# Attention transposed by VectorE in 32x32 blocks with an exchange through DRAM, in a two-layer graph network on one core

## The reference

```python
u = jnp.einsum('bid,bjd->bij', h, h) / temper
a = jax.nn.softmax(u, axis=-1)
delta = a * adjacency_matrix
attn = delta / (jnp.sum(delta, axis=-1, keepdims=True) + 1e-10)
hl = h @ wl.T + b_l
hs = h @ ws.T + b_s
hr = h @ wr.T + b_r
diag_a = jnp.diagonal(attn, axis1=1, axis2=2)
ctx = einsum('bij,bjd->bid', attn * upper, hl) + diag_a[..., None] * hs + einsum('bij,bjd->bid', attn * lower, hr)
o = (ctx - mean) / jnp.sqrt(var + LN_EPS) * g + beta
return relu(o)
```

## Time and profile before

| | |
|---|---|
| median of 3 runs | 1699.22 us (1698.93 to 1699.52) |
| the profiled execution | 1699.16 us, its span 1697.4 us |
| busy share PE, DVE, POOL, ACT | 98%, 84%, 67%, 52% |
| instructions | 34570 |
| TensorE's granted clock, mean | 0.994 of full speed |
| DMA | 97.63 MB in 93905 packets |

### The profile page before, as it was taken

The page is one execution under the profiler, slowest core; times in us unless marked ns, Lnnn a source line. Parts: engine busy times, 40 slices in busy tenths (PEclk is TensorE's granted clock), DMA queues, the critical chain, the costliest instruction groups (busy, mean ns, idle before and its releaser), DMA issues.

```text
span 1697.4 us, 34570 instructions
## 1 busy us (share of the span) xinstructions
PE 1670.7 (98%) x10112; PEld 1652.4 (97%) x10112; DVE 1429.1 (84%) x4496; ACT 882.3 (52%) x2182; POOL 1131.2 (67%) x1798
## 2 busy tenths in 40 slices
PE   7999999999999999999999999999999999999996
PEld 7999999999999999999999999999999999999995
DVE  6888888888888888888888888888888888888887
ACT  4555545554555555455545554555555455545553
POOL 2666676666666666766666666667676666666663
PEclk9999999999999999999999999999999999999998
DMA  4112111111111121111111111111121111111111
GB/s 166 49 52 62 51 57 53 59 53 55 59 54 57 51 61 51 57 52 61 51 57 58 55 57 51 59 54 57 51 62 51 57 57 56 56 52 57 56 46 39
DMA packets 93905, 97.63 MB, mean 58 GB/s; under 512 B 10688, under 2 KB 92864, under 8 KB 93888
## 3 DMA queue, kind: packets, MB, share of 16 engines
q1 hardware_dynamic: 93888, 97.43, 18.5%
HBM read 72.22 MB, written 25.17 MB: 57 GB/s over the span
## 4 chain that ended last, share of the span: by engine, by line
PE 97%; DVE 1%; ACT 0%; issue 0%; DMA 0%; POOL 0%; SPq 0%; DVEq 0%; POOLq 0%; ACTq 0%
PE p_proj L305 71%; PE p_gather L363 16%; PE p_score L299 5%; PE p_gather L385 2%; PE p_attnT L344 2%; PE p_score L337 1%; DMA w_raw<-WT 0%; DVE p_gather L437 0%; DVE proj L462 0%; DVE w L496 0%; DVE stats L406 0%; DVE y L443 0%; ACT w L607 0%; ACT proj_split L587 0%; POOL rstd L671 0%
## 5 line engine op out<-in xcount | busy, mean ns | idle before, releaser
L305 PE MATMUL p_proj<-w,hT_layer 128*128 128x384 f32 x6912 | 1406.6, 344 | 0.2 <-DVE w L496 0.2
L305 PEld LDWEIGHTS p_proj<-w,hT_layer 128*128 128x128 f32 x6912 | 1153.7, 189 | 9.5 <-DVE w L496 0.7
L667 POOL TENSOR_TENSOR attnT_split<-attnT,attnT_split 128x256 fp32r<-128x256 f32 x256 | 189.4, 740 | 449.2 <-DVE rows L481 442.4
L215 POOL TENSOR_TENSOR proj_split<-proj,proj_split 128x768 fp32r<-128x768 f32 x252 | 465.2, 1846 | 5.3 <-issue 5.3
L591 ACT ACTIVATE normed<-gathered,nbias,rstd 128x384 f32<-128x384 f32 x128 | 90.7, 709 | 443.7 <-POOL nbias L675 443.7
L363 PE MATMUL p_gather<-proj_split,attnT_split 128*128 128x384 f32 x1536 | 310.9, 337 | 7.8 <-DVE y L443 4.3
L363 PEld LDWEIGHTS p_gather<-proj_split,attnT_split 128*128 128x128 f32 x1536 | 271.9, 189 | 8.4 <-issue 6.1
L462 DVE TENSOR_TENSOR proj<-p_proj,bias_all 128x768 f32<-128x768 f32 x256 | 243.6, 951 | 6.0 <-PE p_proj L305 5.9
L671 POOL TENSOR_TENSOR rstd<-veps,neg_half 128x1 f32<-128x1 f32 x384 | 210.6, 548 | 49.9 <-DVE neg_mean L420 27.9
L582 ACT ACTIVATE attnT_split<-attnT 128x256 fp32r<-128x256 f32 x256 | 105.0, 410 | 243.5 <-DVE attnT L488 243.5
L299 PE MATMUL p_score<-hT_layer 128*128 128x256 f32 x768 | 215.6, 283 | 5.0 <-POOL hT_layer L707 5.0
(11 more groups left out here) (48 smaller groups left out, 1679.3 us busy)
## 6 DMA issues: line engine op xcount, KB each, us to landing
xt_raw<-xT SPq DMA_DIRECT2D x128, 192.0 KB, 2.4
xn<-x SPq DMA_DIRECT2D x128, 192.0 KB, 2.4
out<-o SPq DMA_DIRECT2D x128, 192.0 KB, 1.9
adj_layer<-adj SPq DMA_DIRECT2D x256, 64.0 KB, 1.9
w_raw<-WT SPq DMA_DIRECT2D x6, 576.0 KB, 7.4
bias_all<-bias SPq DMA_DIRECT2D x2, 576.0 KB, 9.0
gain<-gain_row SPq DMA_DIRECT2D x1, 192.0 KB, 9.6
shift<-shift_row SPq DMA_DIRECT2D x1, 192.0 KB, 9.9
```

The source lines that it names most:

```text
L215: op.tensor_tensor(proj_split[k][:, LO], proj[k][:, UP:LOW + 1, :], proj_split[k][:, HI].bitcast(F32), ALU.subtract).then_inc(s_proj_lo[k], 1)
L305: return nc.tensor.matmul(p_proj[:, which, 0:D], hT[k][:, slot, st, c, :], w[:, k, which, mv, c, :], start=(n == 0), stop=(n == 8))
L667: nc.gpsimd.tensor_tensor(AT_split[k][:, LO], AT[k][:], AT_split[k][:, HI].bitcast(F32), ALU.subtract).then_inc(s_side_lo[k], 1)
```

## The change

The attention is no longer transposed by TensorE, except for the very last graph's layer 2 (`direct`). `mask` is followed on VectorE by `nc.vector.transpose`, which transposes each 32x32 block within `A` in place of the whole, into `A_blocks`; the diagonal is taken from `A` right there. SP stores `A_blocks` to a DRAM scratch and loads it back in four DMAs, one for each group of 32 partitions, with the blocks exchanged, into `AT_whole`. The cut into sides moves from VectorE to GpSimd. Layer 1's normalised rows are still transposed by TensorE, into a bank `p_rows` of their own. Around this, the order of the work changes on every engine: VectorE's output rows go from the end of an iteration (graph i - 3) to just behind layer 1's normalisation (graph i - 4), layer 2's sides and the score matmuls move, and GpSimd's order is new.

The core of the diff:

```diff
+        def direct(i, b):
+            return isinstance(i, int) and b == G - 1
...
+            def store_attn(k, b, slot):
+                done(sp, s_attn_blocks[k], b)
+                sp.dma_start(attn_mem[k][slot], A_blocks[k][:]).then_inc(s_attn_out[k][slot], 16)
+
+            def load_attn(k, b, slot):
+                moved_and_done(sp, s_attn_out[k], b, slot, s_side[k])
+                blocks = attn_mem[k][slot].rearrange("(r a) (s b) -> s a r b", a=B, b=B)
+                for s in range(4):
+                    sp.dma_start(AT_whole[k][s * B:(s + 1) * B, :].rearrange("a (r b) -> a r b", b=B),
+                                 blocks[s]).then_inc(s_attn_in[k][slot], 16)
...
             def iteration(i, p):
                 q = 1 - p
+                if live(i, i):
+                    load_attn(0, i, p)
...
+                if live(i, i - 2) and not direct(i, i - 2):
+                    store_attn(1, i - 2, p)
...
+                if live(i, i - 2) and not direct(i, i - 2):
+                    load_attn(1, i - 2, p)
...
+                if live(i, i + 1):
+                    store_attn(0, i + 1, q)
...
-                    done(pe, s_attn[k], b)
-                    nc.tensor.transpose(p_attnT, A[k][:], ident[:]).then_inc(s_attnT[k], 1)
+                    if k == 1 and direct(i, b):
+                        done(pe, s_attn[k], b)
+                        nc.tensor.transpose(p_attnT, A[k][:], ident[:]).then_inc(s_attnT, 1)
...
-                project_and_score(i, 0, i, p, 1, i - 2, p, i - 3)
+                project_and_score(i, 0, i, p, 1, i - 2, p, i - 3, 4, 16)
...
-                project_and_score(i, 1, i - 2, p, 0, i + 1, q, i)
+                project_and_score(i, 1, i - 2, p, 0, i + 1, q, i, 0, 8)
...
+                done(dve, s_attn[k], b)
+                if not apart:
+                    nc.vector.transpose(A_blocks[k][:], A[k][:]).then_inc(s_attn_blocks[k], 1)
+                nc.vector.tensor_tensor_reduce(diag_scratch[k][:], A[k][:], ident_p[k], 1.0, 0.0, ALU.mult,
+                                               ALU.add, col(rows[k], slot, DIAG)).then_inc(s_diag[k], 1)
...
                 if live(i, i - 1):
                     normalise_layer1(i, q)
+                if live(i, i - 4):
+                    output_rows(i, p)
...
-                if live(i, i - 3):
-                    output_rows(i, q)
...
+            def cut_sides(k, b, slot):
+                gathered_in(pool, s_attn_in[k], b, slot)
+                nc.gpsimd.tensor_tensor(AT[k][:], AT_whole[k][:].unsqueeze(1).broadcast_to([P, 2, N]), sides[:],
+                                        ALU.mult).then_inc(s_side[k], 1)
...
+                if live(i, i - 1):
+                    deviation_layer1(i - 1)
                 if live(i, i - 3) and not by_vector(i, 1, i - 3):
                     low_projections(nc.gpsimd, pool, 1, i - 3)
-                if live(i, i - 4):
-                    deviation_output(i - 4)
-                if live(i, i - 1):
-                    deviation_layer1(i - 1)
+                if live(i, i):
+                    cut_sides(0, i, p)
                 if live(i, i + 1):
                     low_input(i + 1, q)
                 if live(i, i - 2):
                     done(pool, s_attn[1], i - 2)
                 if live(i, i):
                     low_sides(0, i)
+                if live(i, i - 4):
+                    deviation_output(i - 4)
```

More of the change, by code:

```diff
@@ L326, in project_and_score @@
                         last = project_step(k, slot, UP + n // 9, n % 9)
-                    if score and n % 2 == 0 and n // 2 < C:
-                        step = score_step(other, slot_other, n // 2)
-                        if n // 2 == C - 1:
+                    if score and n == first:
+                        done(pe, s_lo[other], b_other)
+                        done(pe, s_diag[other], b_other - 1)
+                    if score and n >= first and (n - first) % 2 == 0 and (n - first) // 2 < C:
+                        step = score_step(other, slot_other, (n - first) // 2)
+                        if (n - first) // 2 == C - 1:
                             step.then_inc(s_parts[other], 1)
@@ L333, in project_and_score @@
                         gather(k, b_gather)
-                    if score and n == 14:
+                    if score and n == last_part:
                         done(pe, s_cross[other], b_other)
@@ L501, in _ @@
             nc.vector.tensor_copy(ident_r[:], ident[:]).then_inc(s_ident_r, 1)
+            for k in range(2):
+                nc.vector.tensor_copy(ident_p[k], ident[:]).then_inc(s_ident_p, 1)
+            dve.wait_ge(s_ident_p, 2)
             dve.wait_ge(s_w[0][UP], 16)
@@ L592, in normalise, with relu_rows @@
                                      scale=rstd[:, which:which + 1]).then_inc(s_rows, 1)
+            def relu_rows(i, b, slot):
+                if isinstance(i, int) and i == 1:
+                    act.wait_ge(s_const, 64)
+                done(act, s_normedT, b)
+                for c in range(C):
+                    last = nc.scalar.activation(relu_T[:, c, :], relu_T[:, c, :], ACT.Relu,
+                                                bias=shift1[:, c:c + 1], scale=gain1[:, c:c + 1])
+                last.then_inc(s_relu, 1)
+                done(act, s_relu, b)
+                done(act, s_self[1], b - 2)
+                nc.scalar.activation(hT[1][:, slot, HI], relu_T, ACT.Copy).then_inc(s_hi[1], 1)
             def finish(i, p):
@@ L619, in iteration @@
                     high_input(i + 1, q)
-                if live(i, i - 2):
+                if live(i, i - 3) and not direct(i, i - 3):
+                    high_sides(1, i - 3)
+                if live(i, i - 2) and not last_graph(i):
                     cross_scores(1, i - 2)
@@ L624, in iteration @@
                     normalise(0, gathered[:], normed[:], s_normed)
-                if live(i, i):
-                    high_sides(0, i)
+                if live(i, i - 2) and last_graph(i):
+                    cross_scores(1, i - 2)
                 if live(i, i - 2):
@@ L635, in iteration @@
                 if live(i, i - 1):
-                    if isinstance(i, int) and i == 1:
-                        act.wait_ge(s_const, 64)
-                    done(act, s_normedT, i - 1)
-                    for c in range(C):
-                        last = nc.scalar.activation(relu_T[:, c, :], relu_T[:, c, :], ACT.Relu,
-                                                    bias=shift1[:, c:c + 1], scale=gain1[:, c:c + 1])
-                    last.then_inc(s_relu, 1)
-                    done(act, s_relu, i - 1)
-                    done(act, s_self[1], i - 3)
-                    nc.scalar.activation(hT[1][:, q, HI], relu_T, ACT.Copy).then_inc(s_hi[1], 1)
-                if live(i, i - 2):
-                    high_sides(1, i - 2)
+                    relu_rows(i, i - 1, q)
                 if live(i, i + 1):
@@ L750, in iteration @@
                     done(pool, s_attn[0], i + 1)
-                if live(i, i - 2) and not last_graph(i):
-                    low_sides(1, i - 2)
+                if live(i, i - 2):
+                    if direct(i, i - 2):
+                        low_sides(1, i - 2)
+                    else:
+                        cut_sides(1, i - 2, p)
                 if live(i, i + 1):
```

120 lines of the change are left out of this document (72 added, 48 removed).

## The result

The changed kernel takes 1765.51 us (median of 4 runs, 1764.82 to 1766.41) against 1699.32 us for the kernel before (4 runs, 1698.93 to 1699.52). The ratio is 1.039, with a 95% interval of 1.0372 to 1.0408: slower, 8.5 us above the forecast of 1757 and inside its range. The span of the profiled execution grew from 1697.4 to 1764.7 us, by 67.3.

What follows compares the result with a forecast made beforehand. TensorE, 98% busy, was taken as the bound before; rings through the new order add 40 us, pass heads 15 and the start 3, taking the 1697.4 us span to 1755. Forecast 1757 us, range 1686 to 1806.

Steps and rivals of the forecast that it cites:

- The ring through the cross copy: From gather through VectorE, GpSimd and ScalarE to TensorE's cross-score matmul: done 9.27 us after S, first-half projection's start, instead of 8.65.
- The stall: TensorE held at layer 1's cross-score matmul for 0.62 us in each iteration, taking 12.66 to 13.28 us.
- the pass heads: Head of each unrolled loop pass: VectorE's 0.31 and GpSimd's 0.18 us losses now count, 30 passes of 0.49, 15 us.
- The second ring: From the late cross copy through layer 1's exponential, mask and layer 2's bias: TensorE's next projection starts at 13.25 us.
- The third: From layer 2's bias through ScalarE's high sides and GpSimd's low sides to layer 1's root: about 13.5, or 13.3 us.
- The iteration: One loop iteration, set by three rings of 13.2 to 13.5 us: taken as 13.3 instead of 12.98, 40 us over 126.
- What TensorE is spared: TensorE's dropped attention transposes: 0.16 us each, two per iteration, 0.32 us, 41 us over 128 graphs as whole possible gain.
- The exchange hides: Store and loads through DRAM land before GpSimd's cut, 1.3 us to spare, layer 2 about as much: costed at nothing.
- The start: Ahead of the loop, the first exchange is uncovered: up to 5 us, taken as 3 us.
- The end: Behind the loop, no added time was forecast.
- TensorE's signs: Cross-score matmul waiting for ScalarE's `cross` some 60 to 80 us in about 125 times; TensorE's busy share about 93%.
- DMA engines: Busy share of the DMA engines with the exchange's pieces at 54 ns each: from 18.5% to about 50%.

Runs made afterwards that it cites:

- e1: Changed kernel with ScalarE's `finish` (the output's normalisation) moved behind layer 1's exponential: 1685.44 us, ratio 0.9918 to the kernel before.
- e8: Changed kernel with the output's deviation put ahead of layer 1's low sides on GpSimd: 1693.46 us, ratio 0.9958 to the kernel before.
- e2: Changed kernel with layer 1's cross-score matmul behind 14 projection matmuls instead of 8: 1765.75 us, ratio 1.0389 to the kernel before.
- e12: e1 with both attention transposes issued on TensorE again, their results unread: 1714.4 us, ratio 1.0085 to the kernel before.
- e3: Changed kernel without the exchange's store and loads, GpSimd cutting from `A_blocks` (output not the reference's): 1751.47 us, ratio 1.0304 to the kernel before.
- e7: e1 with layer 2's weights and constants issued behind the first exchange's loads: 1685.2 us, ratio 0.9912 to the kernel before.
- e5: Changed kernel with the output's statistics back in their old places on VectorE and GpSimd, the exchange kept: 1991.54 us, ratio 1.1732 to the kernel before.
- e10: e1 with every load of the exchange issued twice, first into an unread buffer: 2070.65 us, ratio 1.2188 to the kernel before.

## Why the prediction was right

The direction and the mechanism held, and the terms of the sum came out like this.

- **The ring through the cross copy.** Forecast from S: GpSimd's root 2.08, cut 4.7, cross copy ready 8.9, cross matmul done 9.27. Measured: 2.09 (805.82), 4.64 (808.37), 8.79 (812.52), 9.18 (812.91). The stall, put at 0.62, is 13.42 - 12.765 = 0.66 with the pass heads in it. e1 takes a link out of the ring and e8 makes it 0.74 shorter, and the stall is gone but for the pass heads of e8: shown. The cut, 0.74 us, is a link of the same ring and longer than the stall. No run takes it away from GpSimd in the new order, so it isn't known whether the new order without it would have served.
- **The second ring.** Forecast: the bias ends at 13.1 (the new block transpose is a link here) and the next projection starts at 13.25. Measured: 13.06 and 13.23. e2 shows that it binds by itself when the first is relaxed. The third, through high sides, was not separated.
- **The iteration.** 13.3 and 0.49 per pass of four make 13.42, and 13.42 was measured. In ten iterations of the timeline those at a head take 13.70 and 13.75 and the others 13.23 to 13.40, so a head costs about 0.4, not 0.49, and the rings are 13.33. The 13.3 was picked among three rings put at 13.2 to 13.5, so that it comes out to 0.03 is luck in part. Since the rings hold no attention transpose, this term doesn't depend on the next.
- **What TensorE is spared** was mis-sized: 0.16 us a transpose from the distance between rows, 0.11 by e1 and e12. The step took 0.174 for each of twelve projections, from a run of ten, and put the whole remainder on the transpose. Over the same 22 projections and the cross matmul, TensorE needs 4.05 us before, with one transpose (803.20 to 807.25), and 3.93 in e1, without it (812.39 to 816.32): a projection is 0.176 there, and the transpose 0.12. The whole possible gain was 26 us, not 41, less what the start takes away. The best version, e1, has 14 us of it.
- **The exchange hides** in the loop, as forecast: e3 finds 0.02 us an iteration. The loads' issue took 1.75 us instead of 1.3 (0.44 each, not the 0.33 of an adjacency tile), landing was 1.8. Layer 2's cut does wait, 1.3 to 2.1 us each time in the timeline from 780 to 900, the bulk of the 245.3 us in the list of waits; e3 shows that TensorE doesn't feel it. Here the forecast was wrong: it gave layer 2 about as much cover as layer 1, and named a cut that waits for no DMA as a sign of being right. Layer 1's cut has that cover and waits for none.
- **The start** was put at 3 us and is 8.9, with the exchange itself at 10.3. The bound of 5 us left out that the first store stands behind the weights and biases on the same queue, where its loads wait for it until 19.86; e7, which issues layer 2's later, has its first cut 4.7 us before e1's.
- **The end** was put at nothing and is 3.8. From 1721.53 to the end the granted clock is 0.77 in the mean, against 0.84 before from 1658.02. But e3, without the exchange, has 42.8 us there too, and e1, at 0.83, has 42.5, so neither the exchange nor the clock is the bulk of it. The cause stays open.
- The span was forecast to grow by 58 us and grew by 67.3. The loop was put at 55 for 126 iterations and has 54.6 in 123; the start has 5.9 more than forecast and the end 3.8. That makes the 9.3 us by which the span is off; the median is 0.9 below the profiled execution, which leaves 8.5.
- **TensorE's signs** came out weaker than named: its cross matmul waits 47.4 us by its own row, not 60 to 80 (87.6 by the weight load's), and its busy share is 95%, not 93%.
- **DMA engines** were forecast at 50% and are at 27.8%: 54 ns, a mean that rows of 1536 B make, was too much for pieces of 128 and 512 B (the last section has their times). GpSimd was put at 1320 us and is 1302, VectorE 1397 and is 1400, the cut 0.74 and is 0.741, the block transpose 0.29 and is 0.312.

The books of the loop, all from rows: -26.0 us for the transposes (0.211 x 123), +80.6 for the stall (0.655 x 123), 54.6 together. In the loop the change lost not by its store and loads but by a ring through the order that was written around them; e1, with one instruction moved, gains 14 us with the same exchange and the same cut.

## What to carry to other kernels

When work is moved between engines, walk the ring of every value that the bounding engine waits for, instruction by instruction in the new order; busy shares said that all was well here, and one instruction's place on ScalarE held 80 us. An instruction that nobody waits for soon (an output's normalisation) belongs behind those that the bounding engine waits for. And where an order is partly undone, all engines have to be walked again: e5 lost 230 us by one piece left in its new place, part of it to a clock that fell behind the wait.

## What was not expected of the hardware

- Small DMA pieces took little time each, though not by the byte. The exchange adds 183,600 packets (277,488 less the 93,888 of before: 720 for each of 255 exchanges, 80 of them of 4 B) and about 2,830 us of DMA engine time (27.8% of 16 x 1764.7, less 18.5% of 16 x 1697.4), 15 ns each in the mean. By size, the packets of the changed kernel's trace take 12.1 ns (128 B), 28.8 (512 B) and 78.9 (1536 B) in the mean, so by the byte a piece of 128 B is 1.7 times as dear as one of 512 B. The Trainium skill, "DMA: Bandwidth & Descriptors", Specifications, gives 512 B as the least for full rate, with a read-modify-write below it. The 1.7 agrees with a lower rate below 512 B; a read-modify-write is not seen in these rows. Nor did it matter to the time: a load of 16 KB in 128-byte pieces landed in 1.8 us, less than a 64 KB tile (2.1).
- What such a load costs is its issue, 0.44 us on the queue: in e10 four more of them ahead of each exchange were enough to make every cut wait.
- A transpose of 0.27 us by its row adds 0.11 us between matmuls.
